# Graph network of four layers: node products with the next group's turn ahead of them, and products of zeros in the first weighted sum

## The reference, cut to what matters

```python
x = _layernorm(x + _L0_gnn_ref(x, ...))   # edge attention, 4 heads
x = _layernorm(x + _L1_gnn_ref(x, ...))   # normalised sum over edges
x = _layernorm(x + _L2_gnn_ref(x, ...))   # two sums over edges, two weights
x = _layernorm(x + _L3_gnn_ref(x, ...))   # edge attention, one head
```

```python
ex = jnp.exp(alpha - seg_max[edge_dst])
denom = jax.ops.segment_sum(ex, edge_dst, num_segments=N)
attn = jax.ops.segment_sum(v * alpha[..., None], edge_dst, num_segments=N)
```

## Time and profile before

| | |
|---|---|
| median of 3 runs | 16228.8 us (16222.25 to 16230.81) |
| span of the profiled execution | 18902.1 us |
| PE busy | 11316.2 us (60%) |
| DVE busy | 10279.5 us (54%) |
| POOL busy | 9045.6 us (48%) |
| ACT busy | 4453.3 us (24%) |
| the five node stages together | about 670 us of the span |
| the first weighted sum | about 942 us of the span |

### The profile page before, as it was taken

The page is one execution under the profiler, slowest core; times in us unless marked ns, Lnnn a source line. Parts: engine busy times, 40 slices in busy tenths (PEclk is TensorE's granted clock), DMA queues, the critical chain, the costliest instruction groups (busy, mean ns, idle before and its releaser), DMA issues. The chain is left out here.

```text
span 18902.1 us, 333620 instructions
## 1 busy us (share of the span) xinstructions
PE 11316.2 (60%) x72558; PEld 8597.6 (45%) x72559; DVE 10279.5 (54%) x36111; ACT 4453.3 (24%) x11901; POOL 9045.6 (48%) x10035
## 2 busy tenths in 40 slices
PE   6555555555544666666586666655555665557886
PEld 5333333333333555555475444442223554336776
DVE  9555555555551333333564777773345554777776
ACT  0111111111110222222211342005400112555665
POOL 0555666555562555555674344540263344553332
PEclk9676677666665666666555566765555555557887
DMA  9522222222213222222433698766642777885454
GB/s 378 209 64 64 64 63 64 64 67 61 63 58 64 56 57 57 57 57 57 73 58 36 227 307 283 216 190 215 200 127 69 222 230 222 262 259 178 172 172 140
DMA packets 2144090, 2589.10 MB, mean 137 GB/s; under 512 B 892242, under 2 KB 1761563, under 8 KB 2143939
## 3 DMA queue, kind: packets, MB, share of 16 engines
q1 hardware_dynamic: 1748902, 1741.10, 31.4%
q0 software_dynamic: 353792, 654.90, 11.7%
q10 hardware_dynamic: 41244, 191.56, 2.6%
HBM read 1738.16 MB, written 848.30 MB: 137 GB/s over the span
## 5 line engine op out<-in xcount | busy, mean ns | idle before, releaser
L565 POOL DMA_INDIRECT edges_by_dst<-rec,pos x1568 | 1538.0, 981 | 2027.1 <-DVE rec L500 1577.6
L983 POOL DMA_INDIRECT sc_rows<-src_table,sc_idx x1664 | 1581.7, 951 | 1470.2 <-DVE sc_tp L1081 820.7
L565 POOL DMA_INDIRECT edges_by_cell<-rec,pos x1568 | 1549.2, 988 | 528.9 <-issue 527.4
L1719 PE MATMUL ex_rows<-table,ex_oh 128*128 x6528 | 1177.8, 349 | 830.4 <-DVE ex_oh L1687 406.7
L1805 PE MATMUL gs_part<-gs_rows,gs_oh 128*128 128x192 bf16 x6528 | 1093.2, 329 | 789.5 <-DVE gs_oh L1778 403.9
L1033 PE MATMUL sc_loc<-dst_table,sc_ohT 128*128 x3328 | 772.2, 405 | 1137.7 <-ACT sc_ohT L999 1090.8
L1767 POOL DMA_INDIRECT gs_rows<-rows_by_src,chunk_read_by_src x1088 | 1072.3, 986 | 759.5 <-PE gs_part L1805 441.2
L2213 PE MATMUL at_part<-cell_edge_term,key_in_block 128*66 128x128 f32 x8704 | 1229.6, 306 | 251.0 <-issue 211.5
L1719 PEld LDWEIGHTS ex_rows<-table,ex_oh 128*128 128x128 bf16 x6528 | 755.2, 132 | 1252.9 <-issue 1213.7
L2213 PEld LDWEIGHTS at_part<-cell_edge_term,key_in_block 128*66 128x66 f32 x8704 | 1143.0, 159 | 326.4 <-issue 314.8
L529 DVE SCALAR_TENSOR_TENSOR junk<-rowb,keycol,earlier 128x128 f32<-128x128 f32 (+1 forms) x3136 | 1150.7, 413 | 199.5 <-issue 195.3
(11 more groups left out here) (394 smaller groups left out, 25919.0 us busy)
## 6 DMA issues: line engine op xcount, KB each, us to landing
ex_keys<-src_key_rows SPq DMA_DIRECT2D x1632, 128.0 KB
rows_by_src<-ex_stage SPq DMA_DIRECT2D x1088, 192.0 KB
rowb<-sort_key_rows SPq DMA_DIRECT2D x392, 512.0 KB
ex_keys<-dst_key_rows SPq DMA_DIRECT2D x1088, 128.0 KB
dst_rows_by_src<-patY ACTq DMA_DIRECT2D x1, 104448.0 KB
gs_rows<-dst_rows_by_src SPq DMA_DIRECT2D x544, 192.0 KB
scored_dst_rows_by_src<-patZ ACTq DMA_DIRECT2D x1, 71808.0 KB
scored_rows_by_src<-ex_stage SPq DMA_DIRECT2D x544, 132.0 KB
```

The lines of the kernel that those rows point to most:

```text
L565: nc.gpsimd.indirect_dma_start(out=out, out_offset=bass.IndirectOffsetOnAxis(ap=pos[:, u, k, j:j + 1], axis=0), in_=row, in_offset=None).t ...
L983: nc.gpsimd.indirect_dma_start(out=rows[:, u, j, :], out_offset=None, in_=tabS, in_offset=bass.IndirectOffsetOnAxis(ap=idx[:, u, j:j + 1], ...
L1719: m = nc.tensor.matmul(rows[k][u % 2][r // 2][:, r % 2, 0:W], oh[k][:, u % 2, r * P:(r + 1) * P], t3[:, bass.ds(held[k][u], 1), :].rearran ...
```

## The change

In `node_stage` the turn becomes a function, and PE's order becomes turn 0, turn 1, products 0, turn 2, products 1, turn 3 and so on: before each group's products the next group is turned. The waits of a turn and of a group's products stay what they were. In `weighted_sum` PE issues 24 products of `K.zero` with itself (128x512, bf16) before its loop and two behind each group's products, into a PSUM tile of their own that nobody reads.

```diff
+def occupy(nc, K, bank, times):
+
+    w = bank.shape[1] // P
+    for _ in range(times):
+        nc.tensor.matmul(bank[:, :], K.zero[:, :], bcast(K.zero[:, :], 1, [P, w, P]), start=True, stop=True)
...
             @block.tensor
             def _(pe):
+                def turn(i, u):
+                    g = i * 2 + u
+                    wait(pe, s_fed, g + 1)
+                    wait(pe, s_copy, g - 1)
+                    pe.nop(nofuse=True)
+                    for j in range(4):
+                        m = nc.tensor.transpose(turned[u][0:kin, j * P:(j + 1) * P], fed[:, u, j, :], K.ident[:, :])
+                    m.then_inc(s_turn.sem, 1)
+
                 def body(i, last):
                     for u in range(2):
                         g = i * 2 + u
-                        wait(pe, s_fed, g + 1)
-                        wait(pe, s_copy, g - 1)
-                        pe.nop(nofuse=True)
-                        for j in range(4):
-                            m = nc.tensor.transpose(turned[u][0:kin, j * P:(j + 1) * P], fed[:, u, j, :], K.ident[:, :])
-                        m.then_inc(s_turn.sem, 1)
+                        if u == 0:
+                            turn(i, 1)
+                        elif not last:
+                            turn(i + 1, 0)
                         wait(pe, s_copy, g + 1)
                         wait(pe, s_ev, g - 1)
...
+                turn(0, 0)
                 loop(pe, n, body)
...
+        idle = ctx.enter_context(nc.psum_tensor(f"{name}_idle", [P, 4 * P], F32))
...
                         m.then_inc(s_mm.sem, 1)
+                        occupy(nc, K, idle, 2)
+                occupy(nc, K, idle, 24)
                 loop(pe, n, body)
```

## The result

The changed kernel takes 16382.0 us (median of 4 runs, 16377.7 to 16384.8) against 16225.7 us (16222.3 to 16230.8) beside it: ratio 1.0098, 95% interval 1.0087 to 1.0110. That is 156 us more.

A forecast was written before the change was run, and what follows sets the result against it. The prediction took a ring of PE, ACT and DVE to bound the node stages and POOL the weighted sum. 16228.8 + 172 (node stages) + 170 (weighted sum) = 16571 us, range 16395 to 16665.

The forecast's parts named there:

- The 4 us that I took off in `tables`: Node stage `tables`: some four of the first periods wait for something longer anyway, which hides 4 us of the added time.
- I hold the lower clock for likelier: Weighted sum: the choice of the lower clock, 1.2 GHz, as the forecast, chance 0.54.
- Case 1: Weighted sum at the lower clock, PE becoming the bound: +170 us, kernel 16571 us; the forecast itself, chance 0.54.
- The price of a clock that stays down: Weighted sum: PE takes 2.60 us a group against POOL's 2.26, +148 us in the profiled execution.
- Case 2: Weighted sum: zeros raise the clock, in part or for good; POOL and DVE hold the pace; 0 to +90 us, chance 0.33.
- The allowance for a shorter stage in timed runs: Weighted sum: the stage before may be shorter without a profile, so +148 us was raised to +170.
- the node term: Five node stages: products, eviction, feed and turn run in a row, lengthening periods; +172 us, between 160 and 185.
- Case 3: Weighted sum: the clock rises and the stage gains, term to -127 us, kernel 16274 to 16400 us; chance 0.09.
- Case 4: Node stages: the turn finds its feed done, only the copy wait goes; -122 us, kernel 16107 us with raised clock; chance 0.04.

The follow-up runs named there:

- the first profiled execution: The kernel before the change, unchanged, in its original profile: span 18902.1 us, against a median of 16228.8 us for its runs without a profile.
- the profile at 16197 us: The kernel before the change, profiled again with no edit, also called the second profile: measured 16199 us, span 16197 us.

## Why the prediction missed

**The cause of the loss was right, step by step.** The serial chain of products, eviction, feed and turn is in the trace as described; undoing the moved turn takes the loss away, and so does moving the feed. The median periods came out 6.24 against 6.48 in `lin1`, 4.62 against 4.81 in `lin2`, 6.27 against 6.21 in `lin3`, 3.81 against 4.04 in `proj` and 6.10 against 6.41 in `tables`. Four of the five forecasts are 0.2 to 0.3 too long, mostly for two reasons seen in the timelines: directly behind the turns, eight product slots take 1.81 us where I had 1.96 (their weights start to load at 8575.58, while the turns run until 8576.00), and from the first turn to the products it is 0.83 us (8575.80 - 8574.97) where I had 0.90. The 4 us that I took off in `tables` belonged to a stall of the first profiled execution, which the profile at 16197 us does not have. So the term was +172 and measured +156 (stages' sums) to +160 (the turn alone).

**The step that failed is "I hold the lower clock for likelier".** Case 1 put +170 on the weighted sum, and it measured 0. The clock was up for about half of the stage (0.74 is 0.50 and 1.00 in nearly equal parts). The price of a clock that stays down was right in its mechanism, as the narrow products show (+136 in the stage, +121 in the kernel), and for zeros too high (2.60 us a group against 2.46). Why the clock rose, no run explains beyond this: with one product of zeros a group it did not, with two it did in part, with four nearly throughout. Case 2 was what happened, and its own term was too high too: 0 and not up to +90 (its own numbers, half the groups at 2.60 against 2.26 or 1.95, give 71 or 135, so the 90 was not worked out). It charged those groups as if PE's pace were the stage's at once, and though it had the upper clock's group at 1.34 us (measured 1.27), it did not let PE make up with it before POOL ran out of work.

**The allowance for a shorter stage in timed runs failed as well.** I read the 16% between the profiled execution and the runs as something spread over stages, and raised +148 to +170 for it. The second profile shows that the weighted sum had no part in it, 929 and 928 us. With case 2 at its true 0, the sum would have been 16228.8 + 172 = 16401, 19 us too high, which is the error of the node term and the 3 us by which the kernel before was lower beside the changed one.

**The range** took case 2 from 16401 down to 16395 only, no lower than its sum without error. The node term's own low bound, 160, belonged in it: 16228.8 + 160 = 16389, and still 7 us above the result.

**Rivals.** Case 3, a gain from the raised clock, is excluded for this kernel by the runs with two and four products. It did not come with 116 gathers fewer either; a stage in which POOL surely sets nothing was not run. Case 4 did not come by itself; the runs with the feed ahead made it: the turn found its feed done, and the kernel gained 106 us where case 4 had put 122.

## What to carry to other kernels

When an instruction moves ahead of another on one engine, its wait moves along: follow that wait to what it needs, and ask whether that needs what was just put behind. A turn ahead is worth something only if its input is made a group earlier too; here the two reorderings are -106 us together, and +160 and 0 apart. Products that only hold the clock up are worth nothing in a stage whose pace another engine sets; look at who waits for whom before buying PE speed.

## What was not expected of the hardware

- Products of zeros raised the clock where the kernel's own narrow ones did not: 0.50, 0.50, 0.74 and 0.94 with none, one, two and four products of 512 columns a group, while float32 products of 68 columns left it at 0.50 with PE busy 100% of 1064 us. Nor is it narrow products as such: with the feed ahead, `lin2` has float32 products of 64 columns and turns between them, and the clock there went from 0.50 to 1.00 within the stage (mean 0.78), while `proj`, with PE busy for 64.32 of 71 us, stayed at 0.50. Products of zeros and narrow ones differ in width, type and contents, and no run tells these apart. In these runs PE's busy share alone did not tell its clock. The Trainium skill, "TensorE: Matmul & The Clock Gate", section "What's actually happening", has activity of the array release the halved clock; the runs with two and four agree (0.74, 0.94), and the run with narrow products is one in which a busy PE was not enough.
- A 512-column product of zeros takes its slot plus a tail: 1.06 us for two at the lower clock and 0.59 at the upper, slots of about 0.43 and 0.21 us.
- The same kernel took 16198 and 16221 us on two devices and 18682 to 18723 on a third, in seven runs there. Of the 2705 us between the two profiles of the kernel before, 791 lie in the scoring stage, with POOL busy for about the same time there (1580.66 and 1598.62 us), and some 1024 in the scatters of the edges at the kernel's start (4097 and 5121 us from the first to the last); the weighted sum and four of the node stages do not differ. What was slower there was not found.
